# The first group's expert outputs combined by a gather from HBM instead of one-hot matmuls, in a fused slot-attention and switch-FFN kernel

## What is computed

```python
x = x + slot_attention(layernorm(x), ctx)     # 3 iterations: scores against 32 context rows, softmax over slots, GRU cell
x = x + switch_ffn(layernorm(x))
# switch_ffn, per batch b, 8 experts, capacity 512/8 = 64
logits = t @ Wg;  gates = softmax(logits);  e = argmax(gates);  gate = gates[e]
pos    = how many earlier tokens of the batch chose e       # a token with pos >= 64 is dropped
expert_inputs[e, pos] = t                                   # dispatch
expert_outputs = gelu(expert_inputs @ W1[e]) @ W2[e]        # hidden size 512
output[n] = expert_outputs[e, pos] * gate                   # combine; 0 for a dropped token
```

## Time and profile before

| | us |
|---|---|
| median of 3 runs | 157.21 (157.12 to 157.91) |
| the profiled execution | 158.32 |
| its span, first to last instruction | 156.6 |
| PE busy | 133.4 (85%) |
| DVE busy | 104.1 (66%) |
| ACT busy | 75.2 (48%) |
| POOL busy | 49.1 (31%) |
| granted TensorE clock, mean | 0.965 of full |

### The profile page before, as it was taken

The page is one execution under the profiler, slowest core; times in us unless marked ns, Lnnn a source line. Parts: engine busy times, 40 slices in busy tenths (PEclk is TensorE's granted clock), DMA queues, the critical chain, the costliest instruction groups (busy, mean ns, idle before and its releaser), DMA issues.

```text
span 156.6 us, 2834 instructions
## 1 busy us (share of the span) xinstructions
PE 133.4 (85%) x1063; PEld 100.4 (64%) x1063; DVE 104.1 (66%) x306; ACT 75.2 (48%) x148; POOL 49.1 (31%) x69
## 2 busy tenths in 40 slices
PE   0798899899899899898978608989999999999970
PEld 0594567475575574664735507769998798999740
DVE  2965961698796996997996869908688312163361
ACT  2545670733815824734506564547594136343531
POOL 4732804280862844824901950002300000000000
PEclk9999999999999999999999965599999999999998
DMA  4989980000000000000000000000000000031004
GB/s 134 269 234 345 308 224 1 0 0 0 6 0 0 2 4 0 0 0 2 4 0 0 0 0 0 0 4 0 0 4 2 0 4 0 0 100 38 0 0 134
DMA packets 7857, 7.13 MB, mean 46 GB/s; under 512 B 410, under 2 KB 5796, under 8 KB 7844
## 3 DMA queue, kind: packets, MB, share of 16 engines
q1 hardware_dynamic: 7408, 6.76, 14.7%
q10 hardware_dynamic: 436, 0.20, 0.5%
HBM read 5.91 MB, written 1.05 MB: 44 GB/s over the span
## 4 chain that ended last, share of the span: by engine, by line
PE 54%; DVE 17%; POOL 15%; ACT 6%; issue 3%; DMA 2%; ACTq 0%; DVEq 0%
PE ps L1279 10%; PE ps L1267 10%; POOL d_b L329 9%; PE ps L1185 6%; PE ps L1293 5%; PE ps L1109 5%; PE ps L1101 5%; POOL d_b L324 4%; DVE h L718 4%; ACT z_b L430 3%; DMA x_tok<-in_x_dram 2%; PE ps L977 2%; PE ps L1169 2%; DVE attn L695 2%; DVE rhoT L689 1%
## 5 line engine op out<-in xcount | busy, mean ns | idle before, releaser
L711 DVE SCALAR_TENSOR_TENSOR n_b<-z_b,n_b 128x512 f32<-128x512 f32 x12 | 18.3, 1555 | 1.8 <-ACT n_b L436 1.6
L329 POOL TENSOR_TENSOR d_b<-d_b,h 128x512 f32<-128x512 f32 x12 | 17.3, 1456 | 0.2
L424 ACT ACTIVATE r_b<-ps,half_b 128x512 f32<-128x512 f32 x12 | 7.6, 684 | 19.6 <-PE ps L1109 19.6
L1267 PE MATMUL ps<-h,W_t 128*128 128x128 f32 x128 | 15.9, 277 | 0.9 <-ACT h L466 0.8
L1267 PEld LDWEIGHTS ps<-h,W_t 128*128 128x128 f32 x128 | 15.1, 192 | 2.1 <-issue 1.4
L1109 PE MATMUL ps<-attn,VW 32*128 32x256 f32 x144 | 12.9, 426 | 3.8 <-DVE ps L703 2.5
L900 DVE TENSOR_TENSOR y_lo<-ps,y_hi 128x256 fp32r<-128x256 f32 x8 | 3.4, 425 | 18.1 <-ACT y_hi L541 18.1
L1101 PE MATMUL ps<-h,whhT 128*128 128x256 f32 x48 | 13.5, 403 | 1.1 <-ACT z_b L430 1.1
L389 ACT ACTIVATE h<-h 128x512 f32<-128x512 f32 x12 | 7.4, 630 | 13.0 <-DVE h L718 12.9
L703 DVE SCALAR_TENSOR_TENSOR ps<-r_b,ps 128x512 f32<-128x512 f32 x12 | 7.8, 693 | 8.4 <-ACT r_b L424 8.4
L1109 PEld LDWEIGHTS ps<-attn,VW 32*128 32x128 f32 x144 | 5.6, 182 | 10.9 <-DVE ps L703 4.9
(11 more groups left out here) (166 smaller groups left out, 281.8 us busy)
## 6 DMA issues: line engine op xcount, KB each, us to landing
W_t<-in_L_ffn_W_dram SPq DMA_DIRECT2D x1, 2048.0 KB, 10.1
x_tok<-in_x_dram SPq DMA_DIRECT2D x4, 256.0 KB, 3.8
out_dram<-h SPq DMA_DIRECT2D x4, 256.0 KB, 2.3
n_b<-in_L_xattn_gru_whh_dram SPq DMA_DIRECT2D x1, 192.0 KB, 4.1
n_b<-in_L_xattn_gru_wih_dram SPq DMA_DIRECT2D x1, 192.0 KB, 3.2
n_b<-in_ctx_dram ACTq DMA_DIRECT2D x1, 64.0 KB, 2.9
Wq_t<-in_L_xattn_Wq_dram SPq DMA_DIRECT2D x1, 64.0 KB, 3.7
n_b<-in_L_xattn_Wk_dram ACTq DMA_DIRECT2D x1, 64.0 KB, 3.4
```

What stands on the lines that cost most here:

```text
L329: nc.gpsimd.tensor_tensor(d_b[:, b, :], d_b[:, b, :], h[:, b, :], ALU.mult).then_inc(s["zh"], 1)
L711: v.scalar_tensor_tensor(out=n_b[:, b, :], in0=z_b[:, b, :], scalar=-1.0, in1=n_b[:, b, :], op0=ALU.add, op1=ALU.mult).then_inc(s["c"], 1)
L1267: last = mm(hid_bank[e][:, j * BG * CAP:(j + 1) * BG * CAP], W1_t[:, ex_, j * P:(j + 1) * P], rhs, start=True, stop=True)
```

## The change

For group 0 nothing is combined on PE any more. ACT copies the output of each step to `y_sb` in float32 (`y_out`), SP writes it to `y_rows`, a tensor in HBM with one row of 512 bytes per slot (1024 rows for the two batches), in four transfers of 128 KB. When all four have landed, GpSimd issues eight indirect transfers, one per chunk of 128 tokens, that fetch for every token the row of its slot (`row_of`, the slot plus 512 for the second batch) into `y_tok`. A dropped token's row number is out of bounds, nothing is fetched for it, and `y_tok` keeps the zero of a memset at the start. DVE multiplies with the gate and adds the residual from `y_tok` (`gated_rows`).

Gone from PE are `slot_rows`, `combine` and `back` of group 0, from ACT its `rows_out` and `summed_out`, from DVE its one-hots and low parts. Group 1 goes on as before, with waits renumbered. On DVE, `gated_rows(0)` stands ahead of `y_low(6)` and `gated_rows(1)` ahead of `y_low(7)`.

```diff
--- before.py
+++ after.py
@@ -165,6 +165,10 @@
         x_lo = sb("x_lo", [P, B * C, D], f32r)
         disp = sb("disp", [P, 2, C, N], f32r)
         comb = [sb(f"comb{k}", [P, B, N], f32r) for k in range(2)]
+        y_sb = sb("y_sb", [P, NP, BG, D])
+        y_tok = sb("y_tok", [P, CG, D])
+        row_of = sb("row_of", [P, CG], mybir.dt.uint32)
+        y_rows = nc.dram_tensor("y_rows", [BG * E * CAP, D], f32)
...
@@ -260,6 +266,10 @@
...
+            for k in range(NP):
+                sp.wait_ge(ysb, k + 1)
+                sp.dma_start(y_rows.ap().rearrange("(i k p) d -> k p i d", i=BG, p=P)[k],
+                             y_sb[:, k, :, :]).then_inc(y_put, 16)
...
@@ -336,6 +346,7 @@
...
+            nc.gpsimd.memset(y_tok[:, :, :], 0.0).then_inc(y_zero, 1)
             rho_step(0, 0)
...
@@ -356,6 +367,20 @@
...
+            def fetch_rows(b):
+
+                for n in range(b * C, (b + 1) * C):
+                    nc.gpsimd.indirect_dma_start(
+                        out=y_tok[:, n, :], out_offset=None, in_=y_rows.ap(),
+                        in_offset=bass.IndirectOffsetOnAxis(ap=row_of[:, n:n + 1], axis=0),
+                        bounds_check=BG * E * CAP - 1, oob_is_err=False).then_inc(y_got[b], 16)
+
+            pool.wait_ge(y_zero, 1)
+            pool.wait_ge(idx, BG)
+            pool.wait_ge(y_put, 16 * NP)
+            fetch_rows(0)
+            fetch_rows(1)
...
@@ -468,7 +493,7 @@
...
-                act.wait_ge(srP, b + 1)
+                act.wait_ge(srP, b - BG + 1)
                 nc.scalar.activation(srow[:, b, :], row_bank[b][:, :], ACT.Copy).then_inc(srC, 1)
...
@@ -534,41 +559,43 @@
...
+            def y_out(s):
+                act.wait_ge(yP, s + 1)
+                nc.scalar.activation(y_sb[:, s, :, :],
+                                     y_bank[s % 2][:, 0:BG * D].rearrange("p (b d) -> p b d", d=D),
+                                     ACT.Copy).then_inc(ysb, 1)
+
             def y_high(s):
                 act.wait_ge(yP, s + 1)
-                if s >= 2:
-                    act.wait_ge(accP, s - 1)
+                if s >= NP + 2:
+                    act.wait_ge(accP, s - NP - 1)
...
             def summed_out(b):
-                act.wait_ge(accD, b + 1)
+                act.wait_ge(accD, b - BG + 1)
...
             gelu(0)
-            rows_out(0)
-            rows_out(1)
             x2_out(2)
             x2_out(3)
             gelu(1)
-            y_high(0)
+            y_out(0)
             x2_norm(2)
             gelu(2)
             x_high(2)
             x2_norm(3)
             x_high(3)
-            y_high(1)
+            y_out(1)
             gelu(3)
             dispatched_out(2)
-            y_high(2)
+            y_out(2)
             dispatched_out(3)
-            y_high(3)
+            y_out(3)
             rows_out(2)
             rows_out(3)
             gelu(4)
-            summed_out(0)
-            summed_out(1)
             for s in range(NP, STEPS):
                 if s + 1 < STEPS:
                     gelu(s + 1)
@@ -577,7 +604,7 @@
                 y_high(s)
             summed_out(2)
             act.wait_ge(gt, 2)
-            act.wait_ge(backP, B)
+            act.wait_ge(backP, B - BG)
...
@@ -885,62 +912,70 @@
...
             def combine_hot(s):
-                if s >= 2:
-                    dve.wait_ge(accP, s - 1)
                 g, k = divmod(s, NP)
+                if k >= 2:
+                    dve.wait_ge(accP, k - 1)
                 for b in range(BG * g, BG * (g + 1)):
-                    dve.wait_ge(srC, b + 1)
+                    dve.wait_ge(srC, b - BG + 1)
                     v.tensor_scalar(comb[s % 2][:, b, :], srow[:, b, :], pair_iota[:, k:k + 1], None,
                                     ALU.is_equal).then_inc(cmb, 1)
 
             def y_low(s):
-                dve.wait_ge(yh, s + 1)
-                if s >= 2:
-                    dve.wait_ge(accP, s - 1)
+                dve.wait_ge(yh, s - NP + 1)
+                if s >= NP + 2:
+                    dve.wait_ge(accP, s - NP - 1)
...
+            def source_rows(i):
+
+                cs = slice(i * C, (i + 1) * C)
+                dve.wait_ge(pl, 5)
+                v.tensor_scalar(row_of[:, cs], slot[:, cs], float(i * E * CAP), None, ALU.add).then_inc(idx, 1)
+
+            def gated_rows(b):
+                dve.wait_ge(y_got[b], 16 * C)
+                for n in range(b * C, (b + 1) * C):
+                    c = n - b * C
+                    v.scalar_tensor_tensor(out=res[:, b, c * D:(c + 1) * D], in0=y_tok[:, n, :],
+                                           scalar=gate[:, n:n + 1], in1=x2_tok[:, n, :],
+                                           op0=ALU.mult, op1=ALU.add).then_inc(fin, 1)
+
             def gated_out(b):
-                dve.wait_ge(backP, b + 1)
+                dve.wait_ge(backP, b - BG + 1)
...
-            combine_hot(0)
+            source_rows(0)
+            source_rows(1)
             x2_stats(2)
             x2_stats(3)
             choose(1)
             x2_shift(2)
             x2_shift(3)
-            y_low(0)
-            combine_hot(1)
             place(1)
             dispatch_hot(2)
             x_low(2)
-            y_low(1)
-            combine_hot(2)
             dispatch_hot(3)
             x_low(3)
             scale_logits(1)
-            y_low(2)
-            combine_hot(3)
-            y_low(3)
             combine_hot(4)
+            combine_hot(5)
             y_low(4)
-            combine_hot(5)
-            dve.wait_ge(gt, 1)
-            gated_out(0)
-            gated_out(1)
             y_low(5)
             combine_hot(6)
+            dve.wait_ge(gt, 1)
+            gated_rows(0)
             y_low(6)
             combine_hot(7)
+            gated_rows(1)
             y_low(7)
             gates(1)
-            dve.wait_ge(accD, B)
+            dve.wait_ge(accD, BG)
             v.tensor_copy(oT[:, B - 1, :], acc_bank[BG - 1][:, :]).then_inc(oTv, 1)
             dve.wait_ge(gt, 2)
             gated_out(B - 2)
@@ -1161,10 +1196,7 @@
...
                 pe.wait_ge(pl, 6 * g + 6)
-                if g == 0:
-                    pe.wait_ge(x2c, BG)
-                else:
-                    pe.wait_ge(xeC, B)
+                pe.wait_ge(xeC, B)
...
@@ -1250,8 +1282,6 @@
             logits(0)
             logits(1)
             positions(0)
-            slot_rows(0)
-            slot_rows(1)
             dispatch(0)
             dispatch(1)
 
@@ -1271,8 +1301,10 @@
             def down(s):
                 k = s % NP
                 pe.wait_ge(hidC, 2 * (s + 1))
...
+                if s >= NP + 2:
+                    pe.wait_ge(yl, s - NP - 1)
+                elif s >= 2:
+                    pe.wait_ge(ysb, s - 1)
...
@@ -1284,11 +1316,9 @@
             def combine(s):
...
-                pe.wait_ge(yl, s + 1)
-                if g > 0 and k == 0:
-                    pe.wait_ge(oTs, BG * g)
+                pe.wait_ge(yl, k + 1)
                 for i in range(BG):
-                    pe.wait_ge(cmb, BG * s + i + 1)
+                    pe.wait_ge(cmb, BG * k + i + 1)
...
-                if k == NP - 1:
-                    pe.wait_ge(accD, BG * (g + 1))
-                    pe.sem_inc(accP, 1)
...
             def back(b):
 
                 if b == B - 1:
                     pe.wait_ge(oTv, 1)
                 else:
-                    pe.wait_ge(oTs, b + 1)
-                if b < BG:
-                    pe.wait_ge(srC, B)
+                    pe.wait_ge(oTs, b - BG + 1)
...
@@ -1325,22 +1350,16 @@
             up(2)
             positions(1)
             down(1)
-            combine(0)
             up(3)
             dispatch(2)
             down(2)
-            combine(1)
             dispatch(3)
             down(3)
-            combine(2)
             slot_rows(2)
             slot_rows(3)
             up(4)
-            combine(3)
             up(5)
             down(4)
-            back(0)
-            back(1)
             up(6)
             down(5)
             combine(4)
```

More of the change, by code:

```diff
@@ L209, in slot_attention_and_switch_ffn @@
         out_done = sem("out_done")
+        ysb, y_put, idx, y_zero = (sem(n) for n in ("ysb", "y_put", "idx", "y_zero"))
+        y_got = sems("y_got", BG)
         pool_set, dve_set, fold_set = (sem(n) for n in ("pool_set", "dve_set", "fold_set"))
@@ L1273, in down @@
                 pe.wait_ge(hidC, 2 * (s + 1))
-                if s >= 2:
-                    pe.wait_ge(yl, s - 1)
+                if s >= NP + 2:
+                    pe.wait_ge(yl, s - NP - 1)
+                elif s >= 2:
+                    pe.wait_ge(ysb, s - 1)
                 for i in range(BG):
```

## The result

The changed kernel takes **152.34 us** (median of 4 runs, 151.82 to 153.0) against 157.21 (157.12 to 157.91): 0.968 of before, 95% interval 0.963 to 0.974. The forecast was 150.8 with a range of 149.4 to 154.4; the result is inside that range and outside the narrower 150.0 to 151.7. The profiled execution is 153.0 us with a span of 151.3; before it was 158.32 and 156.6. Later runs give a better base: before 158.1 (29 runs, 157.10 to 158.91), the changed kernel 152.41 (6 runs, 152.07 to 152.92), so a gain of 5.7 us (ratio to the 17 runs of before that stand beside it 0.965, 0.962 to 0.968).

The account below looks back on a forecast made before the run. TensorE (PE) was taken to bound the kernel, almost the whole chain from 94.50 to 150.0 us. Combines 4.47, back 1.02 and dispatch 0.9 gave 6.4 us off 157.2: 150.8 us, range 149.4 to 154.4.

Parts of the forecast that it names:

- PE's pieces: Group 0's combine(0) to (3) and back(0), (1) leave PE's chain: 4.47 plus 1.02 us.
- The dispatch term: Without slot_rows(0), (1), first dispatches start earlier, partly at half clock: 0.9 us gained, not 1.97; bounds 0 and 1.8.
- Rival A: At the first dispatches PE's clock returns sooner, so up(0) comes 1.8 us sooner, not 0.9: 149.9 us; chance 0.12.
- A's own sign, 98: PE's clock back at 1.00 by 98 us, around the first dispatches, would show the sooner clock return.
- 6.4 us: Sum of the PE terms, 4.47 + 1.02 + 0.9, taken off the median 157.2.
- ACT and DVE: Both engines get lighter, ACT by about 2.2 us; thin place up(5), 0.25 us to spare, costed at nothing.
- rival B: PE's work is gone but ACT is the wait behind it, as gelu(4) before up(5): about 152 us; chance 0.08.
- The memset: Zeroing y_tok on POOL ahead of the first rho_step, hidden in a 5.41 us wait there.
- The way through HBM: After down(3): write lands in 2.3 us, eight gathers at 1.2 each, landing 2.3; batch 1 there at 138.5.
- slack for batch 1: Batch 1's gathered rows land at 138.5, due at 141.3 for gated_rows(1) ahead of y_low(7): 2.8 us.
- Rivals C: Gathers at 2.0 us each bring batch 1 3.6 late, losing part of the gain: 154.4 us; chance 0.12.
- D: Gathers run in series on POOL, 3.9 us each, holding y_low(7) and combine(7): about 167.6 us; chance of slower 0.09.

Follow-up runs that it names:

- The fillers: Changed kernel plus unused matmuls and transposes where combine(0), (1), (2) and back(0), (1) stood on PE: 161.34 us; with plain SP transfers replacing its gathers, 155.71 us.

## Why the prediction was right, and where its sizes were off

- **PE's pieces.** Right as a mechanism, since the pieces left the chain and nothing came in their place. Forecast 4.47 + 1.02 = 5.49. From the two chains: combine(0), (1), (2) gave 0.94, 0.92, 0.93, combine(3) with its wait 1.20 (128.94 to 133.88 before, 3.74 after), back 0.83, together 4.82. This is the term that was mis-sized: the prediction took the piece's own row, and left out that the next block's first weight loads had been hidden behind it. The first three combinations and the transposes give 0.2 less than their rows. combine(3) alone gave 0.12 more than its 0.94 + 0.14, because up(5), which had waited behind it, now follows up(4) without a break. The fillers, put where the four others stood, show the 0.2 from the other side. With the 0.4 that the next term was short in that profile, down(7) ended at 143.00 where 141.9 was forecast.
- **The dispatch term.** Forecast 0.9 instead of 1.97, by counting slow and fast matmuls. The first two profiles give 0.49 (102.46 to 101.97; counted from `slot_r` 0.66); the slot rows put back alone cost 1.1; 5.7 less 4.82 leaves 0.9. The size holds about as a mean, and with luck: it assumed that the clock comes back at the same time, which it doesn't from one execution to the next. The reason holds too: at full clock it is zero.
- **Rival A** (clock back sooner) was true in some executions, of both kernels: the second profile of the changed one has up(0) at 101.95, the first at 102.71. The clock was back near 101.2 and 100.5 in the two profiles of before, near 101.3 and 99.4 in those of the changed kernel; A's own sign, 98, was not reached in any of the four. It varies with each execution. Whether the change makes an early return likelier isn't settled: 3 of 29 runs of before are in the group of the higher clock (0.971), and 4 of 10 of the changed kernel (0.975 and up).
- **The level.** The 6.4 us were taken off a median of three runs (four with the one added since, at the same 157.21) that lay 0.9 below that of the next 29. 6.4 and 5.7 are the sizes to compare. Off 158.1 the forecast would have been 151.7, 0.7 below the 152.41 measured, so of the 1.5 us by which it was too low more than half is this base.
- **ACT and DVE** hid what they were said to hide. up(5) followed up(4) without a wait (3.74 for both), so rival B fell. The memset took 0.95 us and held nobody.
- **The way through HBM.** The write landed in 1.8 (forecast 2.3); POOL began its first gather 0.95 after that; a gather cost 1.30 (1.2) and landed in 2.6 (2.3). The forecast had bounded the price of a gather only between 0.21 and 2.3 and took 1.2 from the two POOL operations nearest in kind, so that it came within 0.1 was in part luck. The slack for batch 1 was 2.5, forecast 2.8, and the run with two more gathers, 2.6 late, was still free. Rivals C and D stayed away, but C's mechanism is real: six more gathers turned the gain into a small loss, by way of DVE's list as described.
- **The rule of the Trainium skill** in GPSIMD Engine Reference, 2.1 Instruction dispatch, on a load of some 6 us at the first call of a newly loaded routine: not seen here, though no row shows whether the gather's routine was newly loaded at that point. Between the landing of the write (126.9) and the first gather (127.85) there is 0.95 us, and that gather takes 1.27 against 1.00 for the others.

## What to carry to other kernels

Where one engine is the whole chain, work taken off it pays nearly its rows, less what it hid of the next block (here 0.2 us of weight loads for four of the five pieces), and nothing where another engine is the true bound at full clock. A trip through HBM with a gather is cheap when it has a deadline and meets it: work out when the last row lands (here 1.8 for the write, 0.95 until the first gather, 9.4 until the eighth starts and 2.6 until it lands, 14.8 us from the issue of the last write) and put its consumer as late as its own reader allows. Look in every such kernel for pauses of PE under the name "issue", and of ACT, while GpSimd's gathers run.

## What was not expected

- Pauses of PE of 0.2 to 0.95 us, 3.1 and 4.9 us of delay in sum, inside blocks without waits, with pauses of ACT beside them, only while GpSimd's gathers were in flight and only in two of the kernels that had them. No timed run of these two took under 154.77 and 159.10 us, and with plain transfers of the same size it was gone: 151.26 to 151.79 and 155.34 to 156.91 us. What makes them appear is open.
- A wait of 3.82 us on PE at the very end halved its clock, which made the tail 1.4 us longer, so that the late gathers cost more than their lateness.
- The best version that computes everything is the changed kernel kept busy, 151.97 us: twenty-five matmuls without use, in a pause of PE, make it 0.4 us shorter than 152.41 (ranges 151.63 to 152.08 and 152.07 to 152.92).
